# Two chains of background work change places, and one delay is halved, in a two-layer attention kernel on one core

## The reference

```
L0:  h(0) = rows 0..1023, h(1) = rows 1024..2047; shift, scale and gate from silu(ctx[0:2]) @ ada_w
     x_i  = h(i) + gate * proj(attend(q_i, k_i, v_i))        # self attention inside each half, on mod(ln(h))
     x    = input x + gate * proj(attend(q_i, k_j, v_j))     # each half attends to the other half (crs)
     x    = x + gate * fc2(gelu(fc1(mod(ln(x)))))            # MLP, hidden 1024
L1:  x    = ln(x + out(attend(q, k, v, mask)))               # self attention (sa)
     x    = ln(x + out(attend(q(x), k(ctx), v(ctx))))        # attention to ctx (ca)
     x    = ln(x + w2(relu(w1(x))))
```

## Time and profile before

| | |
|---|---|
| time, three runs | 2379.62, 2380.66 and 2381.78 us, median 2380.66 us |
| the profiled execution | 2380.66 us, span from first to last instruction 2378.8 us |
| PE busy | 2050.1 us, 86% of the span |
| DVE, ACT, POOL busy | 1567.6, 1286.3 and 473.1 us |
| mean granted TensorE clock | 0.911 of full speed |

### The profile page before, as it was taken

One profiled execution on the slowest core, in us unless ns is written; L12 is line 12 of the kernel. 1 busy time (PEld: TensorE's weight loads), 2 busy tenths in 40 slices (PEclk: granted clock), 3 DMA queues, 4 the chain that ended last, 5 costly groups with the idle time before them and its releaser, 6 DMA issues.

```text
span 2378.8 us, 33838 instructions
## 1 busy us (share of the span) xinstructions
PE 2050.1 (86%) x12890; PEld 799.6 (34%) x12890; DVE 1567.6 (66%) x2867; ACT 1286.3 (54%) x2406; POOL 473.1 (20%) x464
## 2 busy tenths in 40 slices
PE   4699998897898899989987947999799999999975
PEld 2423322322232353533523422232244334434424
DVE  3477898685776748357463436886666996796703
ACT  1035675474455576646762714468524775585660
POOL 0013434333131302022022123030303102102100
PEclk7669999997798999999997978699879999999988
DMA  7615223522034202035014232020201102000000
GB/s 148 121 50 107 80 72 106 100 70 62 15 89 84 68 3 66 14 82 100 3 47 91 55 89 62 15 50 6 64 6 45 26 7 57 12 6 13 12 15 11
DMA packets 97305, 126.66 MB, mean 53 GB/s; under 512 B 25293, under 2 KB 81982, under 8 KB 92014
## 3 DMA queue, kind: packets, MB, share of 16 engines
q1 hardware_dynamic: 97134, 124.42, 22.9%
HBM read 89.95 MB, written 24.74 MB: 48 GB/s over the span
## 4 chain that ended last, share of the span: by engine, by line
PE 63%; DVE 12%; ACT 7%; DMA 6%; issue 4%; POOL 3%; SPq 3%; POOLq 0%; ACTq 0%; DVEq 0%
PE ps L1312 18%; PE ps L1266 16%; PE ps L1287 12%; DVE mx L1549 7%; PE ps L1418 5%; PE ps L1371 4%; PE ps L1407 3%; ACT PT L1480 3%; SPq L1078 3%; PE ps L1395 2%; PE ps L1383 2%; DMA QS<-scr 2%; DMA scr<-S 2%; PE ps L1360 1%; ACT big L1522 1%
## 5 line engine op out<-in xcount | busy, mean ns | idle before, releaser
L1480 ACT ACTIVATE PT<-ps 128x512 f32<-128x512 f32 (+1 forms) x2112 | 1099.1, 602 | 726.8 <-PE ps L1266 721.2
L1549 DVE TENSOR_REDUCE mx<-ps 128x1 f32<-128x512 f32 x2048 | 1281.9, 682 | 318.1 <-PE ps L1287 314.9
L1287 PE MATMUL ps<-KS,QS 49*128 49x512 bf16 x2048 | 548.5, 409 | 166.0 <-DVE mx L1549 84.2
L1266 PE MATMUL ps<-QS,KS 51*128 51x512 bf16 (+3 forms) x4224 | 622.1, 392 | 21.6 <-DMA QS<-mr 21.2
L1312 PE MATMUL ps<-PT,Vt 128*32 128x512 f32 (+1 forms) x4224 | 588.2, 629 | 0.0
L1287 PEld LDWEIGHTS ps<-KS,QS 49*128 49x128 bf16 x2048 | 148.5, 95 | 776.2 <-DVE mx L1549 522.2
L1266 PEld LDWEIGHTS ps<-QS,KS 51*128 51x128 bf16 (+3 forms) x4224 | 211.6, 97 | 282.7 <-ACT PT L1480 78.5
L1788 POOL CAST nm<-nm 128x16 bf16<-128x16 f32 x64 | 12.6, 198 | 738.6 <-DVE nm L1562 738.5
L1312 PEld LDWEIGHTS ps<-PT,Vt 128*32 128x32 f32 (+1 forms) x4224 | 84.8, 109 | 151.5 <-issue 147.6
L1407 PE MATMUL ps<-XT,big 128*128 128x256 f32 x512 | 125.2, 395 | 2.5 <-ACT big L1522 1.5
L1418 PE MATMUL ps<-big 128*128 128x256 f32 x512 | 114.7, 382 | 3.4 <-DVE big L1682 2.1
(11 more groups left out here) (106 smaller groups left out, 1168.7 us busy)
## 6 DMA issues: line engine op xcount, KB each, us to landing
scr<-S SPq DMA_DIRECT2D x28, 768.0 KB, 3.5
big<-in_mask_1x1xSxS_ik SPq DMA_DIRECT2D x16, 1024.0 KB, 5.7
QS<-scr SPq DMA_DIRECT2D x32, 384.0 KB, 9.1
KS<-scr SPq DMA_DIRECT2D x24, 384.0 KB, 9.1
QS<-scr SPq DMA_DIRECT2D x32, 256.0 KB, 7.4
ON<-Oe SPq DMA_DIRECT2D x256, 32.0 KB
OD<-scr_r SPq DMA_DIRECT2D x32, 256.0 KB
KS<-scr SPq DMA_DIRECT2D x24, 256.0 KB, 7.2
```

Of the source, the lines that this page charges most:

```text
L1266: z = eng.matmul(ps[0:w, it.bank[j], :], KS[lo:hi, part, pr, col:col + w], QS[lo:hi, part, u.qs, pr, :], start=part == 0, stop=part == 1 a ...
L1287: return eng.matmul(mbank(it)[:, 0:w], QS[lo:lo + MR, 0, u.qs, pr, 128 * it.tq:128 * it.tq + 128], KS[lo:lo + MR, 0, pr, it.lo:it.hi], sta ...
L1480: eng.activation(PT[0:w, it.pt * 4 + 2 * it.pp + j, :], ps[0:w, it.bank[j], :], ACT.Exp, scale=0.25).then_inc(S["exp_done"], 1)
L1549: eng.tensor_reduce(out=mx[:, u.b, c, it.i:it.i + 1], in_=mbank(it)[:, 0:it.hi - it.lo], axis=AX.X, op=ALU.max).then_inc(S["max_done"], 1)
```

## The change

Two kinds of edits in the planner; no instruction is added or taken away. In `post0` for chunks 0 and 1 and in `post` for chunks 2 and 3 the chain of the output projection stands ahead of the chain of the queries (it was behind it). In `ctx_kv` the turning of the loaded rows comes 4 steps after the load instead of 8.

```diff
-            return ([(0, load), (0, lambda: need_kv("ca")), (8, lambda: do_xt("ctx", 4, 0, cols))]
+            return ([(0, load), (0, lambda: need_kv("ca")), (4, lambda: do_xt("ctx", 4, 0, cols))]
...
             if c == 0:
-                return [q_l0(2, 0, 0), out_l0(0, 0)], []
+                return [out_l0(0, 0), q_l0(2, 0, 0)], []
             if c == 1:
                 mark["half_over", 0] = now()
-                return [q_l0(3, 1, 0) + [(0, lambda: l0_weights("crs"))], out_l0(1, 0)], [
+                return [out_l0(1, 0), q_l0(3, 1, 0) + [(0, lambda: l0_weights("crs"))]], [
                     (99, kv_l0(0, 1)), (99, kv_l0(1, 1))]
             if c == 2:
                 return [out_l0(2, 0), q_l0(2, 0, 1)], []
...
                 if c == 2:
-                    return [q_l0(0, 0, 1), out_l0(2, 1) + [(0, lambda: gate_bias(2, I["L0_xattn_mlp_fc2_b"]))]], [
+                    return [out_l0(2, 1) + [(0, lambda: gate_bias(2, I["L0_xattn_mlp_fc2_b"]))], q_l0(0, 0, 1)], [
                         (28, mlp0(2))]
                 if c == 3:
-                    return [q_l0(1, 1, 1), out_l0(3, 1)], [
+                    return [out_l0(3, 1), q_l0(1, 1, 1)], [
                         (32, mlp0(3)), (32, sa_kv(now())), (44, ctx_kv(0, 512, 4, now())), (44, ctx_kv(3, 512, 4, now()))]
```

## The result

The changed kernel takes 2401.05 us in its first 6 timed runs (median) and 2394.0 us over all its 14 executions (median, 2387.79 to 2402.37), against 2381.22 us for the kernel before (6 runs). The ratio, which goes by all 14, is 1.0054, with a 95% interval of 1.0032 to 1.0077: slower by 0.3 to 0.8%. The forecast was 2395.0 us, in a range of 2384 to 2408. The profiled execution took 2393.27 us, 12.6 us more than that of before. Single executions of one kernel spread over some 15 us here, so a term of 2 or 3 us can't be read from the times, and from one pair of traces only where a wait shows it. Two executions among the experiments ran over 11% longer, at a granted clock of 0.72, and are left out of all medians.

A forecast was written before the change was run, and what follows sets the result against it. Time was taken as attention at an even pace plus PE's chain matmuls plus waits, with only waits changing. Terms 17 + 1 - 2.7 - 1 + 0 = 14.3 us on 2380.66 gave 2395.0 us, eight-in-ten range 2384 to 2408.

The forecast's parts named there:

- A: Chunk 0 of the self attention, steps 65 to 104: late queries make PE wait about 12.7 us at step 103; +17 us.
- B: Chunk 1, steps 129 to 192: key chain shrinks the query wait to 0 to 3 us, wait at 175 stays; +1 us.
- C: Chunk 2 of the cross attention, steps 321 to 384: forced MLP burst +1, shorter wait at step 343 -3.7; net -2.7 us.
- D: Chunk 3, steps 385 to 448: forced MLP +1, paced key chain -1, shorter first ctx wait -1; net -1 us.
- E: L1 self attention, steps 529 to 561: ctx wait at step 534 +4, shorter wait for output weights -4; net 0.
- What bounds: Whole kernel: time is attention at its pace plus PE's chain matmuls plus waits; the change touches only the waits.
- The twin in the trace of before: Chunk 2's handover, already output projection first, exactly 128 steps after chunk 0's new order; showed a 12.70 us wait.
- The rival that the wait belongs to the end of the half or to its mask read: Order doesn't make the query wait, so chunk 0's swap costs nothing: 2378 us; 12 in 100.
- B pays in full: Rival for chunk 1: the key chain hides nothing, two query waits of 12 us each, 2406 us; 13 in 100.
- the burst: Step 359, cross attention chunk 2: seven hidden and two output MLP items forced at once, within 3 us of paced; +1 us.
- The rival of the cheaper bursts: Two forced MLPs save 20 ACT table loads and give back 6.4 us at most: 2388.6 us; 8 in 100.
- the halved bounds: Forecast's own range, 2386 to 2402: chunk 0's 12.7 to 18.3 us and the other terms' bounds taken half.

The follow-up runs named there:

- the mask edit: Kernel before with the mask reads of the scan moved 12 steps later and nothing else: 2379.64 us against 2379.77, ratio 1.0000.
- the norm edit: Output projection of chunk 2 in the self attention 2 steps earlier, on the kernel before with the later mask reads: 2380.73 us against 2379.77, ratio 1.0005.

## Why the prediction was right, point by point

One pair of traces can mislead over a term of a few us, so here are the stretches in all traces that have a plan like that of before or of after (in brackets how many; A and B with the early mask scan only), with the difference of the means:

```
steps             plan of before        plan of after         means   forecast
65 to 104  (A)    68.0 to 68.1 (5)      84.4, 85.1 (2)        +16.7     +17
129 to 193 (B)    137.0 to 140.7 (6)    136.0 to 137.2 (3)     -2.9      +1
321 to 385 (C)    138.6 to 140.6 (9)    133.7 to 137.2 (5)     -3.1      -2.7
385 to 529 (D)    330.2 to 333.3 (8)    330.6 to 336.8 (4)     +2.9      -1
529 to 562 (E)    174.3 to 177.9 (8)    171.3 to 172.4 (4)     -3.3       0
```

**What bounds.** Right: PE has the same work, and the change is one of waits.

**A (+17).** Right in place, mechanism and size: +16.4 us in the profiled executions, 17.9 us alone. The twin in the trace of before gave 12.70 us of wait and 26.7 us of chain; measured were 12.80 and 26.8. The rival that the wait belongs to the end of the half or to its mask read is out: it came 128 steps earlier, came again with the old order once the projection was late, and stayed at 10 us without a mask read ahead. The mask read has a part in it, 3 us of the 12.8.
The Trainium skill (TensorE: Matmul & The Clock Gate, Part 1) has an idle array fall to half clock. The trace agrees: the granted clock was 0.52 inside the wait, and beside the wait PE was busy 4.1 us longer for the same matmuls.

**B (+1).** Right in size, in part by luck: +0.2 us, and 1.0000 alone. The key chain hid the query wait as described; 0.78 us were left (forecast 0 to 3):

```profile
462.30 0.59 PE L1287 MATMUL ps<-KS,QS 49*128 49x512 bf16 x3 [0.78 <-DMA QS<-scr]
```

But the 7.04 us wait for the row maxima at step 175, which was to stay, went; the prediction had that as its lower bound of -7. It didn't show in the time, as PE was busy 123.43 us for the same 744 matmuls, before 116.77, at a granted clock of 0.91 after 0.96: 6.5 us of idle less, 6.7 us of busy time more. Over all traces the swap comes out at -2.9 us. The rival "B pays in full" is out.

**C (-2.7).** The step 343 fell to 1.89 us as forecast, and no query wait followed. Steps 359 to 361, with the burst in them, took 32.9 us, 3.6 before; the unpaced MLP had shown 32.3:

```profile
869.54 7.14 PE L1418 MATMUL ps<-big 128*128 128x256 f32 x32 [1.59 <-ACT big L1522]
876.52 7.07 PE L1407 MATMUL ps<-XT,big 128*128 128x256 f32 x32
884.61 7.14 PE L1418 MATMUL ps<-big 128*128 128x256 f32 x32 [1.02 <-ACT big L1522]
891.69 0.39 PE L1287 MATMUL ps<-KS,QS 49*128 49x512 bf16 x2
```

Measured -1.6 us. The rival of the cheaper bursts is out: ACT has 16 table loads ahead of GELU instead of 24 and as many fewer ahead of the exponentials, 16 in all where the rival counted 20, and C shows no gain beyond the 3.7 us of step 343.

**D (-1).** One term was mis-sized: "about 7.5 us of wait remain" at the first ctx turning. It was 13.38:

```profile
1052.07 3.29 SPq L1078 DMA_DIRECT2D ON<-Oe  x4
...
1056.06 0.44 SPq L1078 DMA_DIRECT2D scr<-S  x1
...
1065.13 0.43 SPq L1078 DMA_DIRECT2D xn<-in_ctx  x1
...
1074.03 1.94 PE L1360 MATMUL ps<-identF,xn 128*128 128x128 f32 x8 [13.38 <-DMA xn<-in_ctx]
```

I had carried over the 29 us of the earlier trace rows, where the keys went out as soon as POOL had cut them. In the new place the result of a unit stands ahead in SP's queue: POOL is done at 1049.5, the keys leave at 1056.06, 6.5 us later. From the start of the key projection (1036.39) to the turning 37.6 us pass, where PE's own work fills 24.3 (forecast 29 and some 21.5). The sum came out in this execution (-0.2), at a granted clock of 0.98 from step 385 to 529. Three other traces with the same plan took 332.1, 336.4 and 336.8 us, the last two at 0.95: in the mean D is +2.9, and that the profiled one was level is luck.

**E (0).** Both halves came as described: a wait of 14.37 us at step 534 with none for the row maxima behind it (530 to 545: +4.4, forecast +4), and the wait for the output weights down from 9.99 to 5.77 us (545 to 562: -6.9, forecast -4). The second was larger than forecast. PE was busy for as long in both (68.8 and 68.4 us of steps 545 to 562), so idle time went: 4.2 us of it in the wait for the weights, the rest in shorter ones that I did not trace.

**The sum.** +14.3 forecast, +12.6 in the profiled execution, +12.8 between the medians (all 14 executions), +12.9 by the ratio; the first 6 runs alone gave +19.8. A is shown by its own run and carries the total. The small terms met theirs only in part: by the means B and E came out 3 to 4 us below the forecast and D 4 us above it, and the five means add up to +10.3. One remark on the range: 2386 to 2402 comes out when the halved bounds are added as squares, which the prediction doesn't say; added straight they give some 2376 to 2410.

## What to carry to other kernels

Look for a twin: when a plan is regular, the trace of before may hold the new order already, with its wait and its clock, at a place the change doesn't touch. A chain can be delayed for nothing as long as its data land ahead of their first use (10 steps here); past that, PE stands for the difference. What lies between the two (a key chain here) decides, more than the order. In a queue that is served in order, look at what stands ahead of a transfer: the unit's result, waiting for the attention, held back keys that were ready by 6.5 us (D). And before a term of a few us is called right, look at it in more than one execution.

## What was not expected of the hardware

- Stretches whose plan and work are the same differ by up to 8.5 us between executions: steps 193 to 321 took 266.9 to 275.4 us in nine traces, with a mean granted clock of 0.88 in the shortest and 0.85 in the longest. The wait for the row maxima at step 303 has a part in it (2.87 us before, 7.48 us in the changed kernel).
- Two edits that give nothing alone (ratio 1.0000 each; 1.0005 for the mask edit with the norm edit) give 0.5% together. The larger part of what they do to each other is in PE's busy time for the same matmuls, which goes with the granted clock (0.97 after 0.92 in steps 129 to 193).
